# Eight places instead of four for finished tiles, and two loops that start elsewhere in their instruction block

## The chip, the cores and the metric

The kernel runs on one core of a Trainium2 chip. The core has TensorE (PE), VectorE (DVE), ScalarE (ACT), GpSimd (POOL) and SyncE (SP), each with its own instruction stream, and 16 DMA engines that all of them share. The metric is the device time of one execution in microseconds; the figure for a kernel is the median of its runs.

## The reference

64 x 64 rows of 512 numbers (4096 tokens) go through a small matrix chosen per batch entry and a bias. The result `h` is the input of a mixture-of-experts layer: 16 experts, four chosen per token after a choice of two groups in four, and one shared expert that takes every token. Everything is added onto `x`:

```python
out = jnp.einsum('bct,bcd->bdt', x, w) + b[:, :, None]          # h, with w, b chosen by itok
y = jax.nn.silu(h @ g.T) * (h @ u.T) @ d.T                      # one expert
acc = acc + we[:, None] * y                                     # we is 0 where not chosen
return x + acc + shared
```

## The kernel before, in words

**Tiles.** Work is cut into tiles of 128 rows. 32 tiles (numbers n = 0 to 31) are the tokens in order, for the shared expert. Then come 143 routed tiles (r = 0 to 142, n = 32 + r): each belongs to one expert, and its 128 lanes hold the tokens that chose this expert. Lanes with no token are empty lanes; their index points at a spare row behind the 4096 real ones, in `h_rows` and in `out`. `pad_rows` (line 528) gives tile r the spare rows of set r mod `PAD_SETS`, so that two tiles of one set never have scatters under way together as long as the ring below is as deep as there are sets.

**The path of a routed tile.** POOL gathers its rows (line 574, `tok_ring`, 14 tiles ahead of the scatter). SP moves the rows into a form that can be transposed (`shuffle`, lines 422 to 438, 10 tiles ahead, two tiles at a time: four DMAs at line 434 and one at line 437). DVE transposes (line 1363), ACT copies to `xT_hi` (line 643), DVE makes `xT_lo` (line 1356). PE multiplies by gate and up (12 matmuls into `psGU`), transposes the hidden tile (2, into `psH`), and multiplies by down (6 into `psY`), all by lines 920 and 797. ACT copies `psY` into a place of `y_ring` (`copy_y`, line 707). SP then lets POOL scatter it: it waits for `y_ready` (line 472) and raises `scatter_ok`, and POOL adds the place onto `out` with an indirect DMA (line 579). For a shared tile POOL adds the place with a plain DMA (line 587).

**The ring.** `y_ring` has `YRING` = 4 places. `copy_y` of tile t waits on the semaphore `scattered` of its place until the transfer of tile t - 4 has landed. On ACT it stands ahead of everything else of its step:

```python
copy_y(t + -3, ...)      # lines 744, 745: waits for a free place
copy_xT(t + 1, ...)      # lines 746, 747: the input of PE's next tile
```

so an ACT that waits for a place also holds back `xT_hi` of PE's next tile. The two experts of a token may lie in different tiles, so at the first tile of an expert SP waits until the scatters of the `YRING - 1` tiles before it have landed (lines 466 to 470), before it releases the scatter of that tile.

**The spare rows.** Before the first tile POOL writes zeros to all spare rows (`clear_pads`, line 540): DMAs to `h_rows` and to `out` in turn, two sets in each. The zeros are read from the first 528 numbers of `y_ring`, which DVE clears at the start. `copy_y` of tile 0 therefore waits for every one of the `scattered` semaphores (lines 703 to 706). At about the same time ACT issues the first two copies of `x` into `out` (`copy_x`, line 627; the first two of eight chunks of 1 MiB).

**Loops.** `run_tiles` writes a head of tiles out in line, then a loop of 16 tiles, then a tail. ACT and PE write 46 tiles in line (n = 0 to 45), SP and DVE 48. Each loop's first instruction is put at a given slot of a fetch block of 256 instructions (`SP_HEAD`, `ACT_HEAD`, `DVE_HEAD`); if the code before it ends past that slot, the loop starts in a later block and is entered by a jump. PE gives no slot. Line 117 is the loop statement. Every engine waits on counting semaphores only; there is no planner. The order of work on each engine is the order of the code.

Of the kernel before, what the change touches and what calls it, by code (L numbers as in the profile page):

```python
# [14 lines left out]
P = 128  # L15
B, C, H = 64, 64, 512
N = B * C
NT = N // P
E, TOPK = 16, 4
# [12 lines left out]
NR = (N * TOPK + E * (P - 1)) // P  # L32
NRP = NR + NR % 2
RING = 8
YRING = 4
AHEAD = 14
SHUFFLE_AHEAD = 10
EARLY_AHEAD = 8
# [4 lines left out]
WRING = 2 * RING  # L43
SP_PACK = 4
SP_BITS = 6
PAD_SETS = 4
PADS = PAD_SETS * P
PIECES = 3
PW = EW // PIECES
# [26 lines left out]
LOWS = {21: ((1, 0),), 23: ((1, 1),), 24: ((1, 2),), 26: ((2, 0),), 29: ((2, 1),), 31: ((2, 2),)}  # L76
RAW_LOADS = {15: 1, 16: 2, 23: 3, 31: 4}
WARM_UP = 8
SP_HEAD, ACT_HEAD, DVE_HEAD = 76, 3, 77
N_PAIRS = NT // 2  # L80
LATE_CONSTS = range(3, 8)
X_PAIRS = RING // 2
# [43 lines left out]
def build(nc, x, x_pairs, itok, fside, cond_w, gate_w, expert_bias, ffn_w, out):  # L126
# [4 lines left out]
    with ExitStack() as ctx:  # L131
        def sb(name, shape, dt=F32):
            return ctx.enter_context(nc.sbuf_tensor(name, shape, dt))
# [4 lines left out]
        def sem(name):  # L138
            return ctx.enter_context(nc.semaphore(name))
# [39 lines left out]
        hidT_lo = sb("hidT_lo", [P, 2, I], F32R)  # L179
        y_ring = sb("y_ring", [P, YRING, H])  # L180
        x_duo = x_ring[:].rearrange("p (d w) h -> p d (w h)", w=DUO_TILES).rearrange(
            "p d (j w e) -> p d j w e", j=QUADS, w=DUO_TILES)
        zeros = y_ring[:].rearrange("p r h -> p (r h)")[:, 0:H + E]
# [145 lines left out]
        gathered = [sem(f"gathered{s}") for s in range(RING)]  # L329
        scattered = [sem(f"scattered{s}") for s in range(YRING)]  # L330
        scatter_ok = sem("scatter_ok")
# [31 lines left out]
        def y_round(t):  # L363

            return t.rnd * (RING // YRING) + t.slot // YRING

# [29 lines left out]
        def _(sp):  # L396
# [55 lines left out]
            def routed_step(t, n):  # L452
# [5 lines left out]
                with sp.If(word):  # L458
# [7 lines left out]
                    with sp.If(word & 1):  # L466
                        for d in range(1, YRING):
                            before_t = t + -d
                            sp.wait_ge(scattered[before_t.slot % YRING], (y_round(before_t) + 2) * 16)
                            sp.sem_inc(sp_clear, 1)  # L470
# [24 lines left out]
        def _(pool):  # L495
# [12 lines left out]
            def iota(out_ap, pattern, base, per_partition):  # L508
                link(pool.iota(out_ap, pattern, base=base, channel_multiplier=per_partition,
                               allow_small_or_imprecise_dtypes=True))  # L510
# [6 lines left out]
            def late_const(m):  # L517
# [9 lines left out]
                elif m == 6:  # L527
                    iota(pad_rows[:], [[0, NRP // PAD_SETS], [P, PAD_SETS]], N - N // 2, 1)
                elif m == 7:
# [8 lines left out]
                pool.sem_inc(consts, 1)  # L538

            def clear_pads():  # L540
                for k in range(2):
                    pads = slice(N + k * (PADS // 2), N + (k + 1) * (PADS // 2))
                    pool.dma_start(h_rows[pads, :].rearrange("(s p) e -> p s e", p=P),
                                   zeros.unsqueeze(1).to_broadcast([P, PAD_SETS // 2, H + E])
                                   ).then_inc(scattered[2 * k], 16)
                    pool.dma_start(out[pads, :].rearrange("(s p) e -> p s e", p=P),
                                   zeros[:, 0:H].unsqueeze(1).to_broadcast([P, PAD_SETS // 2, H])
                                   ).then_inc(scattered[2 * k + 1], 16)

            pool.wait_ge(itok_loaded, 16)  # L550
# [16 lines left out]
            entry_consts()  # L567
            pool.wait_ge(blank, 3)
            clear_pads()

            def gather(r):
# [6 lines left out]
            def scatter(r):  # L578
                pool.indirect_dma_start(out[:, :], bass.IndirectOffsetOnAxis(idx_all[:, r:r + 1], 0),  # L579
                                        y_ring[:, r % YRING, :], None, compute_op=ALU.add  # L580
                                        ).then_inc(scattered[r % YRING], 16)
# [33 lines left out]
        def _(act):  # L615
# [4 lines left out]
                load_pair(act, m)  # L620
            act.wait_ge(blank, 2)
            act.activation(warm[:], ones[:, 0:1], ACT.Sigmoid)

            def copy_x(k):
                first = shared_tile(k * X_CHUNK)
                chunk = slice(first * P, (first + X_CHUNK) * P)
                act.dma_start(out[chunk, :], x_rows[chunk, :]).then_inc(x_copied[k], 16)
# [910 lines left out]
```

## Time and profile before

| | us |
|---|---|
| median of 3 runs | 856.63 |
| the three runs | 861.76, 856.63, 852.84 |
| the profiled execution, whole | 860.48 |
| its span, first to last instruction | 858.7 |
| PE busy in it | 827.3 |
| DVE, ACT, POOL busy | 487.0, 406.9, 435.8 |

The granted clock of TensorE averaged 0.994. The profile is one execution, the profiled one, and its time lies near the slow end of the three runs. A row of the time-ordered views begins with the microsecond at which it starts, then its length. A busy PE in these views includes overlap of successive matmuls, so the distance from one tile's first matmul to the next tile's tells more than the busy share.

### The profile page before, as it was taken

Reading aid. Unit: us, or ns where it says so; the run is one execution under the profiler, and the core shown is the slowest. Engines: PE = TensorE matmul, PEld = TensorE weight load, DVE = VectorE, ACT = ScalarE, POOL = GpSimd, SP = SyncE. Lnnn points to the kernel's source line nnn. Section 1 sums busy time; section 2 is a strip of 40 time slices with the busy share of each in tenths; the row PEclk is TensorE's granted clock in tenths of the full one; section 3 lists DMA queues with packets and bytes.
Section 4 is the critical chain, followed back from the end, with each engine's and each line's share of the span. In section 5 each row is a group of like instructions: output and inputs, shape, how many; then the busy total and the mean of one; then the engine's idle time right before and its main releaser. Section 6 shows DMA issues by size and latency. Waiting matters only on the chain.

```text
span 858.7 us, 19565 instructions
## 1 busy us (share of the span) xinstructions
PE 827.3 (96%) x4200; PEld 662.0 (77%) x4201; DVE 487.0 (57%) x1005; ACT 406.9 (47%) x849; POOL 435.8 (51%) x402
## 2 busy tenths in 40 slices
PE   7789999999999999999999999999999999999994
PEld 4458878788888788888888888888888778787883
DVE  4478876654744544754447545656556366364541
ACT  3573357744543444644346444546455354353441
POOL 3351211164365565657655666554574665755333
PEclk9999999999999999999999999999999999999998
DMA  9986857589999999799998999899998999989754
GB/s 323 349 256 181 160 96 195 139 226 249 249 275 189 186 183 196 144 290 242 215 186 154 296 236 210 199 259 191 239 280 190 264 240 221 243 162 192 126 63 62
DMA packets 144826, 179.40 MB, mean 209 GB/s; under 512 B 30602, under 2 KB 103954, under 8 KB 142354
## 3 DMA queue, kind: packets, MB, share of 16 engines
q0 software_dynamic: 37296, 86.95, 50.9%
q1 hardware_dynamic: 106528, 80.45, 35.9%
q10 hardware_dynamic: 834, 10.49, 3.7%
q14 instruction: 150, 1.23, 0.5%
q8 instruction: 18, 0.29, 0.1%
HBM read 82.52 MB, written 65.04 MB: 172 GB/s over the span
## 4 chain that ended last, share of the span: by engine, by line
PE 64%; DMA 8%; issue 8%; SPq 6%; DVE 4%; ACT 3%; POOLq 3%; POOL 3%; ACTq 1%; DVEq 0%
PE psGU L920 39%; PE psY L920 20%; DMA out<-y_ring,idx_all 5%; SPq L434 3%; PE psH L797 3%; DMA tok_ring<-h_rows,idx_all 3%; POOLq L554 3%; POOL out L579 2%; ACT x_ring L740 1%; SPq L437 1%; ACT xT_hi L643 1%; DVE xT_lo L1356 1%; ACT y_ring L707 1%; POOL tok_ring L574 1%; POOL cw_ring L561 1%
## 5 line engine op out<-in xcount | busy, mean ns | idle before, releaser
L920 PE MATMUL psGU<-split_w,xT_hi 128*128 (+1 forms) x1400 | 435.2, 392 | 4.5 <-DVE xT_lo L1356 2.2
L579 POOL DMA_INDIRECT out<-y_ring,idx_all x143 | 232.2, 1624 | 215.3 <-SPq L473 197.1
L920 PEld LDWEIGHTS psGU<-split_w,xT_hi 128*128 128x128 f32 x1400 | 262.7, 188 | 63.3 <-issue 6.5
L920 PE MATMUL psGU<-split_w,xT_lo 128*128 (+1 forms) x700 | 274.4, 392 | 0.0
L920 PE MATMUL psY<-split_w,hidT_hi 128*128 (+1 forms) x700 | 233.0, 414 | 0.2 <-issue 0.2
L755 ACT ACTIVATE aT<-psGU 128x256 f32<-128x256 f32 x175 | 67.2, 384 | 248.0 <-PE psGU L920 219.0
L1356 DVE TENSOR_TENSOR xT_lo<-psT,xT_hi 128x512 fp32r<-128x512 f32 x143 | 98.8, 691 | 151.3 <-ACT xT_hi L643 98.0
L574 POOL DMA_INDIRECT tok_ring<-h_rows,idx_all x143 | 148.3, 1037 | 56.2 <-issue 43.2
L707 ACT ACTIVATE y_ring<-psY 128x512 f32<-128x512 f32 x174 | 103.1, 593 | 133.1 <-PE psY L920 79.6
L920 PEld LDWEIGHTS psGU<-split_w,xT_lo 128*128 128x128 f32 x700 | 131.8, 188 | 29.3
L920 PE MATMUL psY<-split_w,hidT_lo 128*128 (+1 forms) x350 | 138.2, 395 | 0.0
L920 PEld LDWEIGHTS psY<-split_w,hidT_hi 128*128 128x128 f32 x700 | 118.4, 189 | 16.9 <-issue 0.5
L1381 DVE SCALAR_TENSOR_TENSOR aT<-aT,w_ring,psGU 128x256 f32<-128x256 f32 x143 | 66.7, 466 | 84.0 <-ACT aT L755 64.4
L1363 DVE STREAM_TRANSPOSE psT<-x_ring 128x512 f32<-128x512 f32 x143 | 102.5, 717 | 3.8 <-issue 3.8
L643 ACT ACTIVATE xT_hi<-psT 128x512 fp32r<-128x512 f32 x143 | 84.7, 592 | 2.3 <-DVE psT L1363 2.3
L587 POOL DMA_DIRECT2D out<-y_ring x32 | 28.4, 895 | 107.2 <-ACT y_ring L707 107.1
L920 PEld LDWEIGHTS psY<-split_w,hidT_lo 128*128 128x128 f32 x350 | 65.6, 187 | 15.3
L1396 DVE TENSOR_TENSOR split_w<-raw_w,split_w x42 | 51.5, 1227 | 42.4 <-ACT split_w L717 29.8
L1369 DVE TENSOR_TENSOR hidT_lo<-psH,hidT_hi 128x256 fp32r<-128x256 f32 x175 | 72.9, 416 | 1.0 <-issue 0.8
L698 ACT ACTIVATE hidT_hi<-psH 128x256 fp32r<-128x256 f32 x175 | 66.5, 380 | 3.2 <-PE psH L797 1.7
L797 PE MATMUL psH<-ident,aT 128*128 128x128 f32 x350 | 66.7, 272 | 1.1 <-DVE hidT_lo L1369 1.1
L797 PEld LDWEIGHTS psH<-ident,aT 128*128 128x128 f32 x350 | 48.2, 139 | 25.2 <-issue 1.7
(187 smaller groups left out, 403.5 us busy)
## 6 DMA issues: line engine op xcount, KB each, us to landing
x_ring<-tok_ring SPq DMA_DIRECT2D x284, 128.0 KB
raw_w<-ffn_w SPq DMA_DIRECT2D x17, 1536.0 KB, 9.6
h_rows<-tok_ring SPq DMA_DIRECT2D x32, 256.0 KB, 5.8
out<-y_ring POOLq DMA_DIRECT2D x32, 256.0 KB
x_ring<-x_pairs SPq DMA_DIRECT2D x12, 512.0 KB, 5.8
tok_ring<-h_rows,idx_all POOLq DMA_INDIRECT x143
out<-y_ring,idx_all POOLq DMA_INDIRECT x143
x_ring<-x_pairs ACTq DMA_DIRECT2D x4, 512.0 KB, 4.9
```

Source lines behind the costliest of these rows:

```text
L574: pool.indirect_dma_start(tok_ring[:, r % RING, :], None, h_rows[:, :], bass.IndirectOffsetOnAxis(idx_all[:, r:r + 1], 0)).then_inc(gather ...
L579: pool.indirect_dma_start(out[:, :], bass.IndirectOffsetOnAxis(idx_all[:, r:r + 1], 0), y_ring[:, r % YRING, :], None, compute_op=ALU.add) ...
L643: act.activation(xT_hi[:, t.slot % 2, :], xT, ACT.Copy).then_inc(xhi_ready, 1)
L698: act.activation(hidT_hi[:, t.slot % 2, :], psH[:, 0:I], ACT.Copy).then_inc(hidhi_ready, 1)
L707: act.activation(y_ring[:, s, :], psY[t.slot % 2][:], ACT.Copy).then_inc(y_ready, 1)
L755: act.activation(silu[:, t.slot % 2, :], psGU[t.slot % 2][:, 0:I], ACT.Silu).then_inc(silu_ready, 1)
L797: mm = pe.transpose(dst[:, k * P:(k + 1) * P], src[:, k * P:(k + 1) * P], ident[:])
L920: mm = pe.matmul(dst, a[:, slot, c], w(at + col + k * H), start=(k == 0 and a is high and at == 0), stop=(k == parts - 1 and a is low))
L1356: v.tensor_tensor(xT_lo[:, t.slot % 2, :], xT, xT_hi[:, t.slot % 2, :].bitcast(F32), ALU.subtract).then_inc(xT_ready, 1)
L1363: v.transpose(psT[t.slot % 2][:].rearrange("p (k b j) -> p k j b", k=HK, j=QUADS), x_duo[:, t.slot // DUO_TILES, :, t.slot % DUO_TILES, :] ...
L1369: v.tensor_tensor(hidT_lo[:, t.slot % 2, :], psH[:, 0:I], hidT_hi[:, t.slot % 2, :].bitcast(F32), ALU.subtract).then_inc(hidT_ready, 1)
L1381: ins = v.scalar_tensor_tensor(out=hid[:, half, :], in0=gate, scalar=w_ring[:, w_slot, bass.ds(expert, 1)], in1=up, op0=ALU.mult, op1=ALU. ...
```

## The change

`YRING` goes from 4 to 8 and `PAD_SETS` from 4 to 8. There are eight places and eight `scattered` semaphores; `copy_y` of tile t waits for the landing of tile t - 8; SP waits for seven scatters at the start of an expert; there are 1024 spare rows. `clear_pads` makes four pairs of DMAs instead of two, two sets in each as before. `SP_HEAD` goes from 76 to 30 and `ACT_HEAD` from 3 to 5, and ACT gets 36 no-operations near its start.

```diff
-YRING = 4
+YRING = 8
-PAD_SETS = 4
+PAD_SETS = 8
-SP_HEAD, ACT_HEAD, DVE_HEAD = 76, 3, 77
+SP_HEAD, ACT_HEAD, DVE_HEAD = 30, 5, 77
+ACT_NOPS = 36
             def clear_pads():
-                for k in range(2):
-                    pads = slice(N + k * (PADS // 2), N + (k + 1) * (PADS // 2))
+                parts = YRING // 2
+                for k in range(parts):
+                    pads = slice(N + k * (PADS // parts), N + (k + 1) * (PADS // parts))
                     pool.dma_start(h_rows[pads, :].rearrange("(s p) e -> p s e", p=P),
-                                   zeros.unsqueeze(1).to_broadcast([P, PAD_SETS // 2, H + E])
+                                   zeros.unsqueeze(1).to_broadcast([P, PAD_SETS // parts, H + E])
                                    ).then_inc(scattered[2 * k], 16)
                     pool.dma_start(out[pads, :].rearrange("(s p) e -> p s e", p=P),
-                                   zeros[:, 0:H].unsqueeze(1).to_broadcast([P, PAD_SETS // 2, H])
+                                   zeros[:, 0:H].unsqueeze(1).to_broadcast([P, PAD_SETS // parts, H])
                                    ).then_inc(scattered[2 * k + 1], 16)
...
             act.wait_ge(blank, 2)
             act.activation(warm[:], ones[:, 0:1], ACT.Sigmoid)
+            for _ in range(ACT_NOPS):
+                act.nop()
```

## Rows read from the trace of the kernel before

**Rows 1.** The chain in order of time (start us, us, what), an undisturbed tile.

```profile
188.18 2.74 PE psGU L920 x12
...
192.53 2.74 PE psGU L920 x12
```

**Rows 2.** Waits of the engines (us in total, times, longest), those for a place.

```profile
ACT y_ring L707 <- DMA out<-y_ring,idx_all: 17.3, 8, 4.5
...
ACT y_ring L707 <- remote: 3.7, 2, 2.9
```

**Rows 3.** Timeline of ACT (idle time before in brackets): the copy of tile 104.

```profile
685.32 0.60 ACT L707 ACTIVATE y_ring<-psY 128x512 f32<-128x512 f32 x1 [4.45 <-DMA out<-y_ring,idx_all]
```

**Rows 4.** The chain in order of time, 660 to 692 us.

```profile
666.10 1.03 SPq L437
...
677.62 7.15 DMA out<-y_ring,idx_all
...
687.31 3.00 PE psGU L920 x12
```

**Rows 5.** The chain in order of time, 735 to 750 us.

```profile
740.06 1.82 issue
741.88 4.59 PE psGU L920 x12
```

**Rows 6.** Busy time by stretch (last three columns: granted clock, DMA share, GB/s).

```profile
742.80:746.20 3.40, 3.40 (x10) 2.58 (x9) 1.44 (x3) 1.04 (x2) 2.73 (x3) 0.50 1.16 253
```

**Rows 7.** Timeline of PE: first matmuls of routed tiles 102 and 120.

```profile
667.87 0.62 PE L920 MATMUL psGU<-split_w,xT_hi 128*128 x2
...
752.25 0.62 PE L920 MATMUL psGU<-split_w,xT_hi 128*128 x2
```

**Rows 8.** The chain, 262 to 285 us: ACT behind its first L117 branch.

```profile
274.29 3.70 issue
```

**Rows 9.** Timeline of PE: first matmuls of tiles n = 44 and 46.

```profile
275.08 0.62 PE L920 MATMUL psGU<-split_w,xT_hi 128*128 x2
...
284.74 0.62 PE L920 MATMUL psGU<-split_w,xT_hi 128*128 x2
```

**Rows 10.** Instructions of L117 on DVE (ns min/median/max, first to last start us).

```profile
L117 DVEq COMPARE_BRANCH  x8: 47/69/92, 284.5 to 778.2; - x8
...
L117 DVEq BRANCH_PREFETCH_HINT  x7: 39/45/61, 284.6 to 707.5; - x7
```

**Rows 11.** Timeline of POOL: the first of the four clearing DMAs.

```profile
58.76 0.94 POOL L543 DMA_DIRECT2D h_rows<-y_ring  x1 [0.69 <-POOL tile_q L509]
```

**Rows 12.** Busy time by stretch, 59 to 71 us; packets count where they start.

```profile
59.00:60.00 1.00, 0.99 (x6) 0.54 (x4) 0.53 (x1) 1.00 (x3) 1.00 (x2) 1.00 4.09 1059
...
62.00:63.00 1.00, 0.61 (x11) 0.37 (x3) 0.87 (x2) 0.32 (x2) 0.00 (x0) 1.00 0.00 0
...
67.00:69.00 2.00, 2.00 (x12) 1.63 (x11) 1.90 (x8) 0.56 (x2) 0.00 (x0) 1.00 1.02 405
...
70.00:71.00 1.00, 1.00 (x7) 0.81 (x6) 1.00 (x4) 0.00 (x0) 0.00 (x0) 1.00 3.00 987
```

**Rows 13.** Timeline: second copy of x, copy of tile 0, PE's tile 4.

```profile
68.67 0.52 ACTq L627 DMA_DIRECT2D out<-x  x1
...
73.01 0.60 ACT L707 ACTIVATE y_ring<-psY 128x512 f32<-128x512 f32 x1 [0.93 <-PE psY L920]
...
77.15 0.62 PE L920 MATMUL psGU<-split_w,xT_hi 128*128 128x512 f32 x2
```

**Rows 14.** Timeline, start of the kernel: ACT's first copy, a pause of PE.

```profile
7.56 1.26 ACT L651 ACTIVATE tok_ring<-psY,bias_tok 128x512 f32<-128x512 f32 x2 [1.18 <-DVE bias_tok L1031]
...
14.50 1.08 PE L844 MATMUL psGU<-x_ring,cw_ring 64*64 64x512 f32 x7 [1.58 <-POOL cw_ring L561]
```

**Rows 15.** Timeline of DVE: the transpose of routed tile 108.

```profile
679.94 0.72 DVE L1363 STREAM_TRANSPOSE psT<-x_ring 128x512 f32<-128x512 f32 x1
```

**Rows 16.** Waits of SP's queue (us in total, times, longest).

```profile
SPq L470 <- DMA out<-y_ring,idx_all: 47.6, 14, 6.9
```

## The prediction

> **What bounds the kernel now.** First the chain of waits in order of time. From tile 21 on it is almost only PE: a tile's 12 gate-and-up matmuls, 2 transposes and 6 down matmuls, and the next tile's begin 4.35 us later [rows 1]. PE sets the pace of the routed stage; a change of other engines' work is worth only what PE waits for them. So the second view is the distance from one tile's first matmul to the next's. It is 4.35 us nearly everywhere and longer in three places of the routed stage: ACT's entry into its loop, the stretch of routed tiles 103 to 119, and DVE's first steps behind its loop (0.9 us near 790 us, untouched by the change). The third view, the waits, says what ACT waited for in the second place: a place of the ring, whose scatter had not landed [rows 2]. "Remote" is the same wait where the view can't name the transfer; it is the one at 739.8 us. The fourth is the chain around it: SP releases the scatter of tile 100 late, it takes 7.15 us to land, ACT copies tile 104 only then after 4.45 us of idling, and PE starts the next tile 2.0 us after the start of that copy [rows 3, 4].
>
> **Eight places.** From tile 102 to 120 PE needs 752.25 - 667.87 = 84.38 us [rows 7]; 18 tiles at 4.35 [rows 1] are 78.3, so 6.0 us are lost. Of these 3.7 belong to one event: PE pauses for 1.82 us, and then twelve matmuls take 4.59 instead of 2.74 us, in a stretch in which the granted clock is 0.50, the lower of the two levels, 1.2 GHz [rows 5, 6, 1]. With eight places `copy_y` waits for a scatter four tiles, 17.4 us, older; the longest wait was 4.5 us [rows 2]. All 6.0 us go. What is late next is SP, which gives ACT and PE no more reason to wait for it by way of the ring, but still delivers the shuffled inputs. The shuffle of tile 108 was issued by 667.1 us [rows 4] and its transpose began at 679.9 [rows 15], 12.8 us later, the smallest distance that I found in the lagging stretch. PE that no longer waits 6.0 us there eats at most that much; 6.8 us remain for the shuffle to land. I count nothing.
>
> SP gets four waits more at each of the 16 starts of an expert. Only the youngest scatter holds it: 14 such waits took 47.6 us in all [rows 16], and older scatters have landed by then. Passed waits are single sequencer instructions of under 0.1 us like those of [rows 10], so 0.3 us per expert, on SP, which the 12.8 us cover; without that cover it would be 16 x 0.3 = 5 us. Eight sets of spare rows change an index pattern and not the number of gathers or scatters.
>
> **The loop entries.** ACT's first branch of line 117 is followed by 3.70 us in which ACT does nothing [rows 8]. DVE, which has a slot too, gets from its branch to the first instruction of the loop in about 0.1 us [rows 10]. PE feels 284.74 - 275.08 - 8.70 = 0.96 us of ACT's stop [rows 9, 1]; the rest is covered by the time by which ACT's copy is early. If the loop begins where the code has already got to, as DVE's does, the 0.96 us go. Bounds: 0 (the slot isn't met, or the next block is as late) and 0.96. I take 0.96, by DVE's row. SP's new slot can only shorten SP's lag, so by the paragraph above it is worth nothing at PE. The 36 no-operations stand before ACT's first copy, which waits 1.18 us for the bias anyway [rows 14]. At up to 0.07 us each (short sequencer instructions take 39 to 92 ns [rows 10]; an estimate) they take 2.5 us and make that copy up to 1.3 us late; PE's next pause, 1.58 us waiting for POOL [rows 14], takes that in. Nothing counted; at worst 1.3.
>
> **Twice as many spare rows.** This is the part with a price. Four clearing DMAs, issued from 58.76 us [rows 11], write 2 x 528 + 2 x 512 KB, 2.13 MB. They wait: the first copy of `x` starts its packets in the microsecond 59 to 60, 4.09 us of packet time on each engine, and in 62 to 63 still nothing else starts [rows 12]. Then zeros stream at 405 GB/s [rows 12], 5.3 us for 2.13 MB, until about 70.2, where the packets of the second copy of `x` start, 3.00 us of engine time within one microsecond [rows 12] (issued at 68.67 [rows 13]). `copy_y` of tile 0, which must see all the clearing landed, runs at 73.01, just in time for nothing to be lost [rows 13].
>
> With eight DMAs another 2.13 MB stand behind the first. POOL issues them by 65.1 us (four more at 0.75), so they are ready. If they passed ahead of the copy of `x`, the last would land at 70.2 + 5.3 + 0.4 = 75.9. If each engine first carries its packet of that copy, as the first copy's packets went ahead of the zeros at 60 to 63, the last lands 3.0 to 3.3 us later, at about 79.0. From the start of `copy_y` to PE's next tile it is 2.0 us [rows 3, 4], and tile 4 of PE begins at 77.15 [rows 13]. So PE loses 75.9 + 2.0 - 77.15 = 0.8 us or 79.0 + 2.0 - 77.15 = 3.9 us. I take 3.9, since the packets' order at 60 to 63 us is the nearest row and the second copy is issued long before the zeros end. In that part of the kernel PE is the bound and everything behind moves along.
>
> A pause of 3.9 us may also cost the clock. The pause of 1.82 us was followed by 3.4 us at 0.50, worth 4.59 - 2.74 = 1.85 us [rows 5, 6, 1]; that of 1.58 us in the prologue [rows 14] was not, the page's slices show the full clock there. One event on either side is little, so I leave 1.85 us out of the point and put it into the range. The Trainium skill (TensorE: Matmul & The Clock Gate, Part 1) speaks against the change here: by it TensorE's clock follows how busy the engine has been, and an idle stretch leads it back to half rate. By that rule the sum would be 859.3 instead of 857.4. The trace agrees for the one pause at 740 us.
>
> **The sum.** Against the profiled execution: 860.48 - 6.0 - 0.96 + 3.9 = 857.4, and 859.3 with the clock. That execution is 3.85 us above the median of the runs, 856.63, and the runs are 9 us apart. What varies with the luck of transfers in this kernel is the wait for a place, so I suppose that the median execution lacks 3.85 us of the 6.0 and gains only 2.15: 856.63 - 2.15 - 0.96 + 3.9 = 857.4, the same figure by construction. The fastest run, 852.84, says that an execution without such waits costs at most that; less 0.96 plus 3.9 is 855.8, the low end of this case. I forecast **857.4**, own range 855 to 860.
>
> **The rivals.**
> - The zeros are no obstacle (they pass ahead of the copy, or stream faster): 857.4 - 3.9 + 0.8 = 854.3, from the fastest run 852.84 - 0.96 + 0.8 = 852.7. For it: nothing in the rows says who wins at 70 us with both queued. Against: 60 to 63 us. Chance 0.25.
> - The ring was not what mattered: SP and POOL are as late as before, and PE waits in 103 to 119 for a shuffled tile instead of a place. Then the 6.0 (or 2.15 in the median) stay: 856.63 - 0.96 + 3.9 = 859.6. Against it stand the 12.8 us. With it I put the case that ACT's entry is not cured: 858.4. Chance 0.12.
> - Slower: up to eight scatters may now be under way, each transfer takes longer, and SP's wait for the youngest at the start of an expert grows. Nothing bounds the lag but the shuffles. In the dense stretch, 590 to 720 us, there are six such starts; if each wait grows by 3 us the lag grows by 18 us, less the 6.8 us of slack that remain: PE loses 11 us there, 857.4 + 11 = 868. It decides once SP's lag passes the present one by 12.8 us. Against it: the number under way is set by SP's and POOL's pace, which hardly changes. Chance 0.06.
> - Much faster: the median execution loses more to the ring than the profiled one and the zeros are free; under 848 it would need 5 us more than any row shows. Chance 0.03.
>
> **How the numbers follow.** The forecast case has 0.54. The range takes it in with the clock and the zeros' case: 852.0 to 861.0; the slower rival and part of the third are left out. About 1% is what a measurement of this kernel can tell from no change: 848.1 and 865.2 are the limits. Every likely case lies between them: same 0.91, faster 0.03, slower 0.06.
>
> **What would show it.** In the profile after: no wait of ACT's line 707 for a scatter, and 4.35 us from tile to tile in 103 to 119, without a stretch at 0.50 there. About 0.1 us in place of 3.70 behind ACT's first L117 branch. ACT's copy of tile 0 near 79 us, waiting for a DMA, and a pause of PE of nearly 4 us before tile 4, perhaps with the lower clock behind it. The prediction is wrong if that copy comes by 76 us, if PE waits for xT_lo in the routed stage while ACT waited for a transpose, or if line 470 waits clearly more than 47.6 us in all.

## The result, and the profile after

| us | before | changed |
|---|---|---|
| median of 18 runs each | 858.21 | 862.96 |
| lowest, highest | 852.84, 862.82 | 858.10, 866.82 |
| the profiled execution | 860.48 | 860.27 |
| its span | 858.7 | 858.5 |

The ratio is 1.0053, with an interval of 1.0034 to 1.0073: the change costs 4.5 us, 2.9 to 6.3. The forecast was 857.4, its range ended at 861.0, and both are too low. The fifteen further runs of the kernel before put its own median 1.58 us above that of the first three.

The profiled executions hide the loss: by them the two kernels are equal. So the traces are read part by part, and the runs decide on the sum. First the head of the page of the changed kernel (span and instructions; busy time, share and instructions by engine).

```profile
span 858.5 us, 19646 instructions
...
PE 828.0 (96%) x4200; PEld 663.7 (77%) x4201; DVE 487.4 (57%) x1005; ACT 407.0 (47%) x849; POOL 442.9 (52%) x406
```

**The start.** ACT's timeline in the changed kernel (idle time before in brackets): the issue of the second copy of `x`, the copy of tile 0, and one copy of the late ring, to which I come below.

```profile
67.93 0.52 ACTq L631 DMA_DIRECT2D out<-x  x1
...
78.83 0.60 ACT L711 ACTIVATE y_ring<-psY 128x512 f32<-128x512 f32 x1 [7.49 <-DMA out<-y_ring]
...
744.94 0.60 ACT L711 ACTIVATE y_ring<-psY 128x512 f32<-128x512 f32 x1 [2.71 <-remote]
```

PE's timeline in the changed kernel: tile 4, one of its matmul pairs, the first tile behind ACT's entry into its loop, and the two tiles that answer to [rows 7].

```profile
80.73 0.73 PE L924 MATMUL psGU<-split_w,xT_hi 128*128 128x512 f32 x2 [4.15 <-DVE xT_lo L1360]
...
82.53 1.05 PE L924 MATMUL psGU<-split_w,xT_hi 128*128 128x512 f32 x2
...
285.13 0.73 PE L924 MATMUL psGU<-split_w,xT_hi 128*128 x2 [0.60 <-DVE xT_lo L1360]
...
671.69 0.62 PE L924 MATMUL psGU<-split_w,xT_hi 128*128 x2
...
751.65 0.61 PE L924 MATMUL psGU<-split_w,xT_hi 128*128 x2
```

The busy time by stretch in the changed kernel (columns as in [rows 6], the last three being clock, DMA share and GB/s).

```profile
72.00:73.00 1.00, 1.00 (x7) 0.81 (x6) 0.97 (x4) 0.00 (x0) 0.00 (x0) 1.00 2.20 927
73.00:74.00 1.00, 1.00 (x6) 0.84 (x5) 0.78 (x3) 0.00 (x0) 0.00 (x0) 1.00 0.00 0
...
75.00:76.00 1.00, 1.00 (x7) 0.83 (x6) 0.00 (x0) 0.00 (x0) 0.00 (x0) 1.00 1.02 404
...
81.80:85.20 3.40, 3.40 (x10) 2.52 (x9) 3.26 (x9) 0.00 (x0) 0.33 (x1) 0.51 0.91 119
```

This is the picture foretold. The packets of the second copy of `x` start by 73 us in the midst of the zeros; in the next microsecond nothing starts, because each engine is still at work on its big packet; then the zeros go on at 404 GB/s. The copy of tile 0 sees them landed at 78.8 (foretold: about 79.0) and PE pauses for 4.15 us (foretold: nearly 4). Behind it the granted clock is 0.51, the lower of the two levels (the half clock, below), and a pair of matmuls takes 1.05 instead of 0.62 us. From the first matmul of PE's tile 0 (61.94, before 62.69) to that of tile 5 (86.79, before 81.49) the changed kernel needs 6.05 us more: 4.3 up to the start of tile 4, and 1.7 in tile 4, whose twelve matmuls take 4.57 instead of 2.74 us (the chain below).

**The chain** of the changed kernel in order of time (start, us, what): the zeros, PE's tile 4, ACT's entry into its loop, and a pause of PE near 706 us.

```profile
63.26 15.39 DMA out<-y_ring
...
80.73 4.57 PE psGU L924 x12
...
279.26 3.59 issue
...
705.22 0.88 issue
706.10 1.64 PE psY L924 x6
707.75 0.39 issue
708.13 3.04 PE psGU L924 x12
```

ACT's entry still has 3.59 us in which ACT does nothing, as the 3.70 of [rows 8], and PE still pauses for 0.60 us. This part of the change had no effect.

**The ring.** The waits of the changed kernel (total us, times, longest): the two of the copies into the ring and the one of PE for its input.

```profile
ACT y_ring L711 <- DMA out<-y_ring: 7.5, 1, 7.5
...
PE psGU L924 <- DVE xT_lo L1360: 5.2, 3, 4.1
...
ACT y_ring L711 <- remote: 2.7, 1, 2.7
```

And that of SP's queue which answers to [rows 16].

```profile
SPq L471 <- DMA out<-y_ring,idx_all: 46.0, 12, 6.3
```

The 17.3 us in eight waits of [rows 2] are gone. One wait is left, the "remote" one at 744.94, and the trace's semaphore records say that it is not for a place. By its position it is the copy of routed tile 117. The scatter that last read its place is that of tile 109, issued at 722.83, and its 16 landings are on record by 729.23. What changes just before the copy, at 744.91, is PE's semaphore `down_done`, though the matmuls that raise it had ended at 743.14: the change is recorded 1.77 us late. PE's next tile did not feel it.

The same is true of the "remote" wait of the kernel before, on which the prediction put 3.7 of its 6.0 us:

```profile
739.80 0.60 ACT L707 ACTIVATE y_ring<-psY 128x512 f32<-128x512 f32 x1 [2.87 <-remote]
```

The first instruction of this copy waits for `down_done` and is through at 739.71, after a change of that semaphore at 739.69, 3.99 us behind the end of PE's matmuls (735.70). The wait for the place comes behind it and takes nothing. In the copy at 685.32 [rows 3] it is the other way round: `down_done` is passed at 681.82, and the place holds the copy for 3.4 us more. That one is a wait for a scatter, the one at 739.80 is not. Changes of `down_done` in the routed stage that come more than 1 us late stand in nine of the sixteen traces of this document, with four places and with eight. Why they are late is not shown.

From 671.69 to 751.65 PE needs 79.96 us against 84.38 before. 1.9 of these 79.96 are the pause near 706. It begins with a transpose on DVE, of the input of the tile that PE should have begun at about 706.3:

```profile
703.26 0.73 DVE L1367 STREAM_TRANSPOSE psT<-x_ring 128x512 f32<-128x512 f32 x1 [2.46 <-issue]
```

This instruction waits for the semaphore of the shuffle, whose DMAs SP had issued from 685.91 to 689.07. Only some of their landings are on record, the last at 700.18, so a late shuffle is the likely cause and not a shown one. Inside the routed loop no other of the sixteen traces has such a wait of over 1.3 us. Behind it PE's sequencer, which is otherwise ahead of its matmuls, has two reads of a tile's word (L915) in the open, 0.86 and 0.99 us. So 84.38 - 79.96 + 1.9 = 6.3 us were not lost again. 3.7 of them are the pause near 740, which was not the ring's. About 2.3 are the ring's, 1.9 of them at two tiles, and 0.3 come from a slightly quicker tile (see the end).

(The prediction numbers the tiles of PE's rows two too low: PE's first 36 matmuls are three tiles. Its times and distances are not touched by that, and below I name times.)

### The profile page after: what moved, and what is told of

Read it like the earlier page. It is cut to its first block, busy times and chain, and to the rows that moved or that the text cites. A ratio compares the mean times of both kernels' runs of the same rounds, so it can differ in the third digit from the quotient of the medians.

```text
span 858.5 us, 19646 instructions
## 1 busy us (share of the span) xinstructions
PE 828.0 (96%) x4200; PEld 663.7 (77%) x4201; DVE 487.4 (57%) x1005; ACT 407.0 (47%) x849; POOL 442.9 (52%) x406
## 4 chain that ended last, share of the span: by engine, by line
PE 81%; issue 4%; DVE 3%; POOLq 3%; ACT 3%; POOL 2%; DMA 2%; ACTq 0%; SPq 0%
PE psGU L924 50%; PE psY L924 26%; PE psH L801 4%; POOLq L556 2%; DMA out<-y_ring 2%; ACT x_ring L744 1%; DVE xT_lo L1360 1%; POOL cw_ring L563 1%; ACT xT_hi L647 1%; DVE x_ring L1342 1%; ACT y_ring L711 1%; POOLq L563 0%; DVE entry L1340 0%; POOL out L581 0%; POOL h_rows L545 0%
```

## Experiments

Each kernel was measured beside the kernel before on one chip, in a series of runs; kernels "of the same series" stood beside one another. "Tile" without a kind counts from the first shared tile, as in [rows 13].

**The price of the spare rows by itself.** The kernel before, with eight sets of spare rows and everything else as it was.

```diff
-PAD_SETS = 4
+PAD_SETS = 8
```

> The kernel before with PAD_SETS = 8 and nothing else: four places, the same four clearing DMAs with twice the bytes. Theory A (the spare rows alone cost what the changed kernel lost at the start: the copy of tile 0 waits until about 78.7 us, PE pauses 4.2 us before its tile 4 and then runs 3.4 us at 0.50): 6 us slower than before, ratio 1.007, and the waits for a place stay. Theory B (the loss comes from eight places or from the moved loops; the spare rows are worth under 2 us): ratio under 1.003.

Measured (seven runs): 865.62 against 859.53, ratio 1.0070 (1.0045 to 1.0095), so 6.0 us. The copy of tile 0 on ACT, PE's tile 4, and the waits for a place:

```profile
79.14 0.60 ACT L707 ACTIVATE y_ring<-psY 128x512 f32<-128x512 f32 x1 [6.49 <-DMA out<-y_ring]
```

```profile
81.03 0.74 PE L920 MATMUL psGU<-split_w,xT_hi 128*128 128x512 f32 x2 [3.15 <-DVE xT_lo L1356]
```

```profile
ACT y_ring L707 <- DMA out<-y_ring,idx_all: 20.0, 7, 4.7
```

The doubled clearing alone makes the whole loss and more, and the ring's waits stay (20.0 us in seven, before 17.3 in eight). In this execution the pause was 3.15 us and the clock held (1.00 from 80.5 to 84 us). DVE's work of line 1002, which the pause had put off, held up the transposes of tile 4 instead, by 0.8 us. Measured from tile 0 to tile 5 as above, the start cost 4.1 us in it.

**The no-operations that were not there.** ACT's entry had not changed at all, which raised the question whether they are in the program. With a hint they are certain to be:

```diff
-                act.nop()
+                act.nop(hint='pad')
```

> The changed kernel with its 36 no-operations kept in the program (they are dropped from it as it was built, so ACT's loop was still entered by a jump, 3.59 us). Theory A: ACT's entry now takes about 0.1 us as DVE's does, PE's 0.9 us there go, so 0.9 us less than the changed kernel, ratio to before 1.0045; the no-operations cost nothing at the start. Rival: the entry still takes over 3 us wherever the loop begins, and the ratio is that of the changed kernel, 1.0053, or more by up to 1.3 us.

Measured: 861.50 against 859.53, ratio 1.0015 (0.9986 to 1.0044). The head of its page, and ACT's first copy within the loop:

```profile
span 862.4 us, 19682 instructions
```

```profile
284.71 0.60 ACT L711 ACTIVATE y_ring<-psY 128x512 f32<-128x512 f32 x1 [2.47 <-issue]
```

19682 - 19646 = 36: the no-operations are in now and were not in the changed kernel. (A kernel further down has `ACT_NOPS = 0` and also 19646 instructions.) ACT's entry takes 1.93 us from branch to loop instead of 3.59, not the 0.1 expected, but that is short enough: PE does not pause there. PE's first tile comes at 63.75 instead of 61.94. That this is the price of the no-operations is not shown: in the traces without them it comes anywhere from 61.51 to 63.56. The pause behind the zeros is 3.36 instead of 4.15 us, again with the half clock behind it. From tile 0 to tile 5 PE needs 24.03 instead of 24.85 us. With the 0.8 us at the entry that is 1.6 us; the ratio is 3.3 us lower than that of the changed kernel, whose interval just overlaps this one.

**Zeros that nobody waits for, eight places and four.** The first 528 numbers of the ring, from which the zeros are read, are places 0 and 1, the first that ACT needs. Moved to the last two places, with a semaphore of their own, only the copy of tile 6 (with four places: 2) and the first gather wait for them. The other waits on `scattered` count one landing less; those lines are left out here.

```diff
-        zeros = y_ring[:].rearrange("p r h -> p (r h)")[:, 0:H + E]
+        zeros = y_ring[:].rearrange("p r h -> p (r h)")[:, (YRING - 2) * H:(YRING - 2) * H + H + E]
...
-                                   ).then_inc(scattered[2 * k], 16)
+                                   ).then_inc(pads_cleared, 16)
...
-                if n == 0:
-                    for k in range(1, YRING):
-                        act.wait_ge(scattered[k], 16)
-                act.wait_ge(scattered[s], (y_round(t) + 1) * 16)
+                if n == YRING - 2:
+                    act.wait_ge(pads_cleared, 16 * N_CLEARS)
+                if n is None or n >= YRING:
+                    act.wait_ge(scattered[s], y_round(t) * 16)
```

The changed kernel with this edit:

> The changed kernel, but the zeros are read from the last two places of the ring and the clearing has a semaphore of its own, so the copy of tile 6, not of tile 0, waits for it (and the first gather). Same bytes, same DMAs. Theory A (the loss at the start is the wait of the copy of tile 0 alone): PE's tile 4 begins at about 77.2 us, no 0.50 there, 6 us less than the changed kernel: 857, ratio to before 0.9985. Theory B (the extra 2.1 MB cost by their traffic, or the rest of the change costs): ratio 1.003 or more.

The kernel before with it (four places, four sets):

> The kernel before (four places, four spare sets) with the same edit: zeros in the last two places, own semaphore, the copy of tile 2 waits for the clearing. It lost nothing there, so theory A: ratio 1.000 to before, and the difference of e3 to this one is what eight places are worth in the median, 1 to 2 us by the medians of the two kernels (4.75 = 6.0 - 1.25), 6 us by the profiled execution of before. Rival: over 0.5% from before, in either sense, if the semaphore's move itself does something.

Measured in the series of the two above: 856.01 and 857.86 against 859.53, ratios 0.9973 (0.9945 to 1.0001) and 0.9986 (0.9958 to 1.0014). With eight places the copy of tile 0 on ACT, and PE's first tile behind ACT's entry:

```profile
72.72 0.60 ACT L712 ACTIVATE y_ring<-psY 128x512 f32<-128x512 f32 x1 [0.93 <-PE psY L925]
```

```profile
280.17 0.73 PE L925 MATMUL psGU<-split_w,xT_hi 128*128 x2 [0.82 <-DVE xT_lo L1361]
```

There is no pause at the start, and the clock stays full there. Between the two ring sizes stand 1.85 us, near the 2.15 that the prediction gave the median and far from the 6.0 of the profiled execution. Both kernels were measured once more in another series, with as many runs each.

> e3 again. Theory A (eight places are worth what the four-place kernels' traces lose between tiles 102 and 120, 2 to 6 us): at least 1.5 us under e13, ratio to before about 0.997. Rival (nothing in the median): within 0.7 us of e13.

> e4 again. Theory A: ratio to before 0.9985 to 1.000, at least 1.5 us over e12. Rival: within 0.7 us of e12.

Measured: 856.43 and 857.70 against 860.05, ratios 0.9963 (0.9943 to 0.9983) and 0.9980 (0.9956 to 1.0004). Eight places with zeros out of the way are faster than the kernel before. The ring alone: 1.27 us here; over the 24 runs of each ring size in both series the means differ by 1.9 us (0.4 to 3.4, by resampling the runs). The traces show where: from routed tile 100 to 109 PE needs 1.7 to 6.0 us more than nine undisturbed tiles in five of the six traces with four places (the sixth, with 0.0, is the one with the slow loop turns below), and nothing more in the ten with eight. What four places cost in a bad execution, from the chain of the second four-place run:

```profile
666.30 9.09 DMA out<-y_ring,idx_all
...
677.46 4.60 PE psGU L921 x12
```

Here a late scatter (9.09 us) makes ACT and then PE wait, and the twelve matmuls behind take 4.60 instead of 2.74 us at half clock. The four-place trace of the first series has two pauses of 0.41 and 0.76 us for the ring and no half clock behind them: what the ring costs differs from execution to execution.

**Who delays the zeros.** The changed kernel with the second copy of `x` issued two tiles later:

```diff
-X_COPIES = {1: 1, 5: 2, 9: 3, 13: 4, 17: 5, 21: 6, 25: 7}
+X_COPIES = {3: 1, 5: 2, 9: 3, 13: 4, 17: 5, 21: 6, 25: 7}
```

> The changed kernel with the second copy of x issued by ACT two tiles later (step 3 instead of 1), so it doesn't stand in the DMA engines while the zeros are written. Theory A (of the pause of 4.2 us, 3.3 come from the packets of that copy, which go ahead of the zeros): the last zeros land near 75.5 to 76 us, PE's pause is about 1 us and no half clock follows; 5 us less than the changed kernel, ratio to before 0.9995. Rival (the engines share, the bytes alone decide): the pause shrinks by less than 1.5 us, ratio 1.0035 or more.

and, of the same series, the changed kernel with the loop starts of before, without no-operations:

```diff
-SP_HEAD, ACT_HEAD, DVE_HEAD = 30, 5, 77
-ACT_NOPS = 36
+SP_HEAD, ACT_HEAD, DVE_HEAD = 76, 3, 77
+ACT_NOPS = 0
```

> The changed kernel with the slots of before (76, 3) and without the no-operations. Theory A (the moved loop starts did nothing for PE, since ACT's was still entered by a jump and SP's 2 us are covered by its distance ahead): SP's entry about 3.2 instead of 1.2 us, the time that of the changed kernel, ratio 1.005 to 1.006. Rival (SP's entry or its longer body matters): more than 1 us away from the changed kernel.

Measured: 860.34 and 862.83 against 857.49, ratios 1.0017 (0.9991 to 1.0044) and 1.0043 (1.0018 to 1.0069). The later copy is better by 2.3 us in the mean (1.0 to 3.4). With it, by stretch, and then the copy of tile 0 and PE's tile 4:

```profile
72.00:73.00 1.00, 1.00 (x6) 0.82 (x5) 0.97 (x10) 0.42 (x2) 0.00 (x0) 1.00 1.02 405
73.00:74.00 1.00, 1.00 (x6) 0.84 (x5) 0.97 (x5) 0.00 (x0) 0.00 (x0) 1.00 1.01 400
```

```profile
76.77 0.60 ACT L711 ACTIVATE y_ring<-psY 128x512 f32<-128x512 f32 x1 [4.34 <-DMA out<-y_ring]
```

```profile
78.66 0.73 PE L924 MATMUL psGU<-split_w,xT_hi 128*128 128x512 f32 x2 [1.01 <-DVE xT_lo L1360]
```

Now the zeros stream without a break, the copy comes 2.4 us earlier than with the old loop starts (79.13), PE's pause falls from 3.57 to 1.01 us, and the half clock behind it is gone. I had expected 5 us from it and got half of that. The first clearing DMA is issued at 59.09 here, at 58.88 with the old loop starts and at 57.92 in the changed kernel. Counted from there the copy of tile 0 comes after 17.7, 20.3 and 20.9 us. So the big packets cost the zeros 2.6 to 3.2 us, close to the 3.0 to 3.3 that I took; the rest of the delay is the volume of the zeros. The Trainium skill (DMA: Bandwidth & Descriptors, Queues, rings and completion order) says that an engine takes packets from its queues in turn, one whole packet at a time. By that rule one big packet gets ahead of the zeros, whoever queued first. The trace agrees: with the copy issued at 67.93 its packets go in between, and 0 GB/s start in the microsecond from 73 on.

The old loop starts measured the same as the new ones (1.0043 and 1.0053). SP then takes up to 5.61 us around its loop, where it takes 0.4 with the new slot, and PE feels nothing of either: no gain from SP's slot is seen, as foretold.

**A dose of it.** The kernel before with twelve sets of spare rows:

```diff
-PAD_SETS = 4
+PAD_SETS = 12
```

> The kernel before with PAD_SETS = 12 alone: another 2.1 MB of zeros beyond e1. Theory A (the zeros are written at 405 GB/s and the copy of tile 0 waits for the last): the wait ends 5.3 us later than in e1, PE's pause is 8 to 9 us, 11 to 12 us slower than before, ratio 1.013. Rival (a fixed cost of touching the start): the ratio of e1, 1.007.

Measured (four runs): 871.41 against 857.49, ratio 1.0126 (1.0069 to 1.0183), 10.8 us. Its PE's tile 4, and the stretch around it:

```profile
85.83 1.22 PE L920 MATMUL psGU<-split_w,xT_hi 128*128 128x512 f32 x2 [9.63 <-DVE xT_lo L1356]
```

```profile
80.00:90.20 10.20, 4.38 (x10) 3.47 (x11) 4.92 (x12) 2.67 (x6) 1.78 (x2) 0.50 0.55 111
```

Four more sets move the copy of tile 0 from 79.14 to 83.93. The clearing began at 59.08 there and at 57.54 here, so counted from its start they add 6.3 us for 2.13 MB, 1.0 more than the 5.3 by which the prediction priced that volume; what the 1.0 is, is not shown. By the runs they add 4.8 us, from wide intervals. The half clock now lasts 10.2 us, of which PE is busy for 4.38.

**A loop start that meets the code.** For ACT 36 or 46 no-operations don't put the loop into the block that the code has reached; slot 226 does.

```diff
-SP_HEAD, ACT_HEAD, DVE_HEAD = 30, 5, 77
-ACT_NOPS = 36
+SP_HEAD, ACT_HEAD, DVE_HEAD = 30, 226, 77
+ACT_NOPS = 0
```

With eight places and the zeros last:

> e3 (eight places, zeros in the last two) with ACT's loop put at slot 226 and no no-operations at all: the code before it should end near slot 211 of the same block. If that is so: ACT's entry takes about 2 us or less as in e2 and e5, PE's 0.9 us at its tile 46 go, and nothing is late at the start (in e2 and e5, with no-operations, PE's first gate-up began at 63.8 us, in the others at 61.6 to 63.3). About 1 us under e3, ratio to before 0.996. Rival: 226 lies in another block than the code reaches, the entry takes over 3 us, ratio of e3, 0.9973.

With four places and the zeros last (slot 230):

> e4 (four places, zeros in the last two) with ACT's loop at slot 230, where its code ends near 215: the same cure with four places. What eight places are worth is e9 less this one, both cured at the entry: 1.9 us by e3 against e4, so ratio to before 0.998 here and 0.996 in e9. Rival: eight places are worth nothing in the median and the two are within 0.5 us.

With eight places, and DVE's loop at slot 4 too:

> e9 with DVE's loop at slot 4 instead of 77. DVE stands still for 4 us in its first step behind the loop (PE loses 0.9 to 1.8 us near tile 162 in every trace). Theory A (the tail's first instructions lie in a block that isn't there yet, and where the loop ends in its block decides): the stop moves or shrinks, PE's 1 us there goes, 1 us under e9. Rival (it comes from the end of the loop whatever the slot), or the entry of DVE now costs what it did not before (0.14 us): same as e9 or up to 1 us more.

Measured in one series, six runs each, against 858.70: 872.11, ratio 1.0156 (1.0118 to 1.0193); 867.43, 1.0097 (1.0060 to 1.0134); 875.78, 1.0200 (1.0165 to 1.0234). The chain of the first at ACT's second turn, and that of the third at DVE's entry:

```profile
414.79 3.99 issue
...
421.04 3.01 PE psGU L925 x12
```

```profile
282.68 4.41 issue
```

The entry itself is what was wanted, 0.36 us. But now every turn of ACT's loop is slow: 1.63, 3.99, 5.44, 4.93, 4.79, 4.54 and 3.33 us behind the branches, where slots 3 and 5 have 0.4 to 2.7, and PE pauses at nearly every one. The loop's body has 612 instructions in the built program. From slot 5 it touches three blocks of 256, from slot 226 four. That this count decides is a guess: SP's loop in the changed kernel with the old starts (606 instructions from slot 76) touches three and turns as badly, up to 5.61 us. All three kernels with ACT's new slot lose at each turn what the old one lost once. DVE's slot 4 is an entry by a jump (4.41 us, PE's tiles there take 6.59 and 6.05 us); it removes the stop behind DVE's loop (4.75 us from tile to tile in the first of the three, 5.28 in the kernel before) and brings one of 5.43 two tiles earlier.

**The entry, shortened by no-operations that are kept.** Zeros last, eight places, and 46 kept no-operations, first all at the start:

```diff
-ACT_NOPS = 36
+ACT_NOPS = 46
-                act.nop()
+                act.nop(hint='pad')
```

> e3 with ACT's no-operations kept, 46 of them, since its code is ten instructions shorter. If the three findings add up (clearing off the path, eight places worth 1.9 us by e3 against e4, ACT's entry no longer felt by PE, 0.9 us): 0.9 us less than e3, about 855.5 where before has 859.5, ratio 0.9955 to 0.9965, clear of 1. Rival: the entry was worth nothing in the median and the ratio is e3's, 0.9973.

then four in each step of the prologue from step 3 on, where ACT idles:

```diff
-ACT_NOPS = 36
+ACT_NOPS = {m: 4 if m < 14 else 2 for m in range(3, 15)}
...
-            for _ in range(ACT_NOPS):
-                act.nop()
...
+                for _ in range(ACT_NOPS.get(m, 0)):
+                    act.nop(hint='pad')
```

> e12 with 46 no-operations kept, but spread over steps 3 to 14 of ACT's prologue, where it waits for PE, and the loop at slot 5. Theory A: the entry takes about 2 us, PE loses nothing at tile 46, 0.9 us under e12. Rival (the shifted code or the no-operations give it back at the start, as e5 seemed to): PE's first gate-up begins at 63.5 us or later and the time is e12's.

Measured: 856.29 against 857.49, ratio 0.9983 (0.9956 to 1.0010), and 856.46 against 860.05, ratio 0.9952 (0.9931 to 0.9973). The second's page head, and PE's first tile behind ACT's entry:

```profile
span 852.2 us, 19679 instructions
```

```profile
279.22 0.72 PE L925 MATMUL psGU<-split_w,xT_hi 128*128 x2
```

No pause at the entry, which takes 2.66 us in place of 3.59. With the no-operations at the start PE's first tile comes at 63.85, with them spread at 62.38; without them it comes at 62.40 and 62.15 with eight places and last zeros, so a price at the start is suggested and no more. The last kernel beats the one before by 4.1 us (2.3 to 5.9), the lowest ratio here. Against the same kernel without no-operations of the same series it is 0.5 us better in the mean (between 1.6 better and 0.6 worse): the entry's own worth is not shown in the runs.

## Why the prediction was wrong, point by point

**Spare rows: the mechanism right, the size short by the clock.** The step that failed is the one that weighed the half clock: "One event on either side is little, so I leave 1.85 us out of the point." The pause of 4.15 us was followed by the lower clock, and the twelve matmuls behind it took 4.57 instead of 2.74 us, 1.83 more. In the traces of this start the clock stayed up behind pauses of 1.01 and 3.15 us and fell behind those of 3.36, 3.57, 4.15 and 9.63, each once. Of the 15 pauses of 1.82 to 3.15 us in all traces from PE's first tile on, ten were followed by the lower level and five were not, so the length of a pause does not decide alone. The foretold pause of 3.9 was longer than all of these, and the row that stood for it [rows 5, 6] had a pause half as long. By the Trainium skill (TensorE: Matmul & The Clock Gate, Part 1) an idle stretch leads the clock back to half rate, and by that rule the sum was 859.3. The trace agrees for the four longest. By the runs the doubled clearing alone costs 6.0 us, against 3.9 foretold; the 1.85 left out would be nearly all of the difference. How often the runs pay it is not shown: the traced execution of that kernel did not, and was as long as its median.

The landing was foretold for 79.0 and came at 78.83. Counted from the first clearing DMA that is 20.2 foretold (58.76 in its row) and 20.9 measured; without the big packets 17.1 and 17.7. The term holds within 0.7 us.

**Eight places: about the right size, by a wrong reading.** The runs give 1.9 us (0.4 to 3.4), the prediction took 2.15 for the median. But it read all 6.0 us of the profiled execution as waits for a place. 3.7 of them followed the late change of `down_done` at 739.69, which eight places do not touch; taken out, 2.3 are left. It set 3.85 of the 6.0 aside as the luck of the profiled execution, without knowing which, and that this came so close was luck as well. "No wait for a scatter" came true. SP's wait of line 470 (now 471) is 46.0 us against the 47.6. The shuffle was given 6.8 us of slack and came out as the likely cause of the one pause near 706. The slower rival did not show.

**ACT's entry: not delivered.** A second term that failed: 0.96 us were taken off in full. The 0.96 us stayed (0.60 of it shows as a pause in the row above) because the 36 no-operations were not in the program; the second rival took this case in, with 0.12 for both. Had they been in, the entry would have fallen to 1.93 us, not to 0.1, and PE's pause there would have gone all the same. "By DVE's row" was a poor yardstick: the entry where the code has got to, slot 226, takes 0.36 us, but ACT's turns behind it take 1.63 to 5.44, while DVE's loop, entered in 0.14, turns in at most 2.8. The Trainium skill (Runtime: NRT & Kernel Launch, Instruction fetch mechanics) says that an engine holds two blocks of code, fetches ahead in sequence only, and stops on a taken branch whose target it doesn't hold. The trace agrees for the entries of ACT and DVE (1.9 to 4.4 us against 0.14 to 0.36). The turns do not follow from it alone: a body of three blocks turned in as little as 0.39 us.

**The base.** 856.63 was the median of three runs; eighteen say 858.21. With the three corrections the sum is 857.4 + 1.85 + 0.96 + 1.58 = 861.8, against 862.96 measured. By differences, which need no base: 6.0 for the clearing less 1.9 for the ring is 4.1, against the measured 4.5 (2.9 to 6.3). The forecast had a difference of 0.8. The clearing was 2.1 short, the entry 0.96, the ring 0.25, together 3.3; what is left lies within the intervals.

**Why the profiled execution said "equal".** At the start it lost 6.05 us. It did not have the pause near 740, 3.7 us, nor the waits for a place, about 2.3, and lost 1.9 near 706. Its tiles were 0.016 us quicker over most of the span, which over 100 tiles is 1.6 us, and PE's first tile began 0.75 us earlier. So most of what hid the loss belongs to the two executions and not to the kernels.

## What to carry to other kernels

A buffer that also serves as the source of a start-up transfer is not free until that transfer has landed: before you enlarge the transfer, put its source where the buffer is used last. Price a pause of PE with what the clock does behind it, and take that price into the point when the pause is longer than one that was followed by the lower level. When a wait has no named releaser, look which semaphore changed last before you put it down to the cause at hand. When a profiled execution is far from the median, ask for each term whether it belongs to the kernel or to that execution; and look in the page's instruction counts whether what the source adds is in the program at all.

## What the runs showed of the hardware

**Two paces of one code.** A tile, with the same instructions, takes 4.353 us in some executions and 4.337 in others, steadily, over a hundred tiles; a change from one to the other comes only at a pause of PE. In the traces: before 4.353 until its pause at 740 us, then about 4.335; the changed kernel 4.337 until 790, then 4.353; with the zeros last, four places took 4.337 in the first series and 4.353 in the second, and eight places the reverse. It is worth up to 2.4 us of 150 tiles and follows none of the edits. I have no cause for it.

**Turns of a loop.** Behind its loop's branch ACT waits 0.4 to 2.7 us with the loop at slot 3 or 5, and up to 5.44 us at slot 226 or 230. SP waits 0.4 us with its loop at slot 30 and up to 5.61 at slot 76 with eight places. The loop gives a hint of its start in every case. The cause is not shown.

**A scatter's landing.** Indirect DMAs of the same size landed 7.15 us (kernel before) and 9.09 us (four places, zeros last) after their issue in the dense stretch.

**A semaphore that is late.** PE's `down_done` changed 3.99 us after the end of the matmuls that raise it (kernel before, 739.69), and 1.77 us after it in the changed kernel (744.91); ACT started 0.11 and 0.03 us behind these changes. PE itself ran on.
